# Two graph layers on one core: a deeper pipeline in the edge pass, another split of the last node update, and fewer waits of GpSimd on TensorE

## The reference

```python
# layer 0
msgs = z[dst] @ Wd + z[src] @ Ws + edge_weight[:, None] * ww + bm
agg = segment_max(msgs, dst)                       # 0 where a node has no edge
x = layernorm(x + (relu(z @ W1a + agg @ W1b + b1) @ W2 + b2))
# layer 1
h = x @ node_fc_W + node_fc_b
alpha = segment_softmax(sum(h[src] * h[dst], -1), dst)
beta = segment_softmax(sigmoid(relu(edge_mlp(edge_attr)) . W2 + b2), dst)     # three gates per edge
h_att = segment_sum(alpha * (h[src] @ node_att_W)) / 3
h_rel = segment_sum(sum_m beta_m * (h[src] @ rel_att_W_m)) / 3
h_out = where(deg > 0, relu(concat(h_att, h_rel) @ out_fc_W + out_fc_b), h)
x = layernorm(x + gate * h_out + (1 - gate) * x)   # gate = sigmoid(x @ gate_W + gate_b)
```

## Time and profile before

| what | value |
|---|---|
| median of 3 runs | 2750.39 us (2747.92 to 2776.14) |
| the profiled execution | 2757.0 us, of which the span 2755.3 us |
| mean granted clock of TensorE | 0.803 |
| busy shares | PE 67%, PEld 41%, DVE 49%, ACT 40%, POOL 60% |
| edge-run pass, gathers at line 209 | 40.35 to about 1203 us |
| edge pass, gathers at line 462 | 1342.83 to about 2613 us |

### The profile page before, as it was taken

How to read it: one execution, slowest core, us unless ns; L and a number is a source line. 1 busy time by engine, 2 the same in 40 slices (tenths; PEclk the granted TensorE clock), 3 DMA queues, 4 the chain that set the end, 5 groups by cost and what they waited for, 6 DMA issues and landing times. The chain is left out here.

```text
span 2755.3 us, 43228 instructions
## 1 busy us (share of the span) xinstructions
PE 1841.2 (67%) x9891; PEld 1141.9 (41%) x9891; DVE 1341.2 (49%) x5207; ACT 1113.2 (40%) x3305; POOL 1654.1 (60%) x1718
## 2 busy tenths in 40 slices
PE   4677777667677775656567776667766667766774
PEld 3222222222222221114356665656655556655674
DVE  4555555554344444324545454445444455444459
ACT  1233333333333333323444444444444444444455
POOL 3756666666677776636445655555555665555535
PEclk7789888988888898777777777777778877787777
DMA  8433333333333333323311212121112122122213
GB/s 232 171 102 124 105 120 107 122 105 124 100 122 103 109 120 108 122 63 93 111 41 51 50 51 52 48 51 52 48 51 52 51 52 52 48 53 51 51 43 99
DMA packets 115983, 235.04 MB, mean 85 GB/s; under 512 B 32909, under 2 KB 68230, under 8 KB 106422
## 3 DMA queue, kind: packets, MB, share of 16 engines
q0 software_dynamic: 52832, 109.39, 16.2%
q1 hardware_dynamic: 56522, 97.21, 9.6%
q10 hardware_dynamic: 6540, 27.42, 2.8%
HBM read 166.01 MB, written 67.89 MB: 85 GB/s over the span
## 5 line engine op out<-in xcount | busy, mean ns | idle before, releaser
L462 POOL DMA_INDIRECT d_region<-d_h,d_region x784 | 747.2, 953 | 552.0 <-issue 238.3
L209 POOL DMA_INDIRECT acc<-d_src_product,b_region x784 | 779.5, 994 | 383.8 <-issue 204.8
L642 PE MATMUL banks<-acc,b_region 64*128 64x512 f32 x1176 | 345.5, 695 | 296.6 <-ACT gate_col L747 159.6
L850 DVE SCALAR_TENSOR_TENSOR acc<-b_region,acc 128x128 f32<-128x128 f32 x784 | 270.4, 345 | 362.9 <-DMA acc<-d_src_product,b_region 333.1
L1570 DVE TENSOR_TENSOR acc<-acc,banks 128x160 f32 x784 | 252.2, 322 | 327.3 <-remote 133.0
L642 PEld LDWEIGHTS banks<-acc,b_region 64*128 64x128 f32 x1176 | 106.2, 204 | 493.2 <-ACT gate_col L747 186.0
L1369 PE MATMUL banks<-d_region 128*128 128x128 f32 x1568 | 303.2, 352 | 9.2 <-issue 9.2
L1372 PE MATMUL banks<-d_region,pick 128*128 128x128 f32 x1568 | 289.2, 344 | 4.7 <-issue 4.5
L1372 PEld LDWEIGHTS banks<-d_region,pick 128*128 128x128 f32 x1568 | 274.0, 260 | 6.6 <-issue 6.5
L1369 PEld LDWEIGHTS banks<-d_region 128*128 128x128 f32 x1568 | 266.3, 255 | 16.4 <-issue 11.0
L861 DVE SCALAR_TENSOR_TENSOR acc<-acc,b_region 128x128 f32<-128x128 f32 x784 | 269.2, 343 | 0.0
(11 more groups left out here) (262 smaller groups left out, 2471.5 us busy)
## 6 DMA issues: line engine op xcount, KB each, us to landing
d_runs<-acc SPq DMA_DIRECT2D x48, 1024.0 KB
acc<-ea ACTq DMA_DIRECT2D x25, 1024.0 KB
acc<-d_src_product,b_region POOLq DMA_INDIRECT x784
d_region<-d_h,d_region POOLq DMA_INDIRECT x784
d_region<-d_rel SPq DMA_DIRECT2D x49, 256.0 KB
hT<-xT SPq DMA_DIRECT2D x7, 448.0 KB, 6.9
d_src_product<-acc SPq DMA_DIRECT2D x7, 448.0 KB, 4.2
acc<-xrow SPq DMA_DIRECT2D x1, 3136.0 KB
```

Source lines behind the costliest of these rows:

```text
L209: pool.indirect_dma_start(self.rows[:, s, j, :], None, d["B"], bass.IndirectOffsetOnAxis(self.idx[:, k:k + 1], 0)).then_inc(self.gathered[ ...
L462: pool.indirect_dma_start(rows[:, s, :], None, table, bass.IndirectOffsetOnAxis(idx[:, s:s + 1], 0)).then_inc(gathered[q], 16)
L642: last = nc.tensor.matmul(bank[4 + n % 2 * 2 + h][:, :], wf[h * DE:(h + 1) * DE, m * P:(m + 1) * P], ea[h * DE:(h + 1) * DE, u % (2 * UC), ...
L850: nc.vector.scalar_tensor_tensor(rows[:, s, j, :], wwb, wgt[:, k:k + 1], rows[:, s, j, :], ALU.mult, ALU.add).then_inc(ch, 1)
```

## The change

It touches five places.

1. The edge pass: the sums of group q stand at the head of TensorE's round, and everything ahead of them works one group further ahead (rows of q+5, scores of q+4, spread of q+3, weights of q+2). ScalarE and VectorE follow, but ScalarE's rescale stays at q, and VectorE's gate weights stay at q+1 and its additions at q. The weights `wts` get four buffers where there were two, and to make room `rel` is held as bf16, which is converted in the tables phase.
2. The gathers of the edge pass: `LAG` is 4 where it was 3, and the wait on turned weights in the middle of a group is gone.
3. The gathers of the edge-run pass: the two looks are gone; `LEASH` is counted in groups and stands for the same wait.
4. The last node update: ScalarE scales one product, GpSimd adds only the bias, VectorE adds three products, and ScalarE does the norm with the mean and root that VectorE prepares.
5. The tables phase: one more copy on VectorE.

In the diff below the third and fourth hunks from the end are TensorE's and VectorE's rounds of the edge pass, the last two ScalarE's part of the last node update.

```diff
...
             pool.wait_ge(rows_turned, it * NG + (NG + q - LAG + 1 + NG))
             pool.wait_ge(idx_ready, it * NG + (NG + q + 1))
             pool.wait_ge(rows_used, it * NG + (NG + q + 1))
-            gathers(q, range(0, GJ // 2))
-            pool.wait_ge(weights_turned, it * NG + (NG + q - LAGW + 1 + NG))
-            gathers(q, range(GJ // 2, GJ))
+            gathers(q)
...
-LAG = 3
-LAGW = 6
+LAG = 4
-LEASH = 4
-LOOKS_FROM = 12
+LEASH = 8
...
-                u = g // 2
+                if g >= LEASH + 2:
+                    pool.wait_ge(dt, (g - LEASH) // 2)
                 for j in range(GJ):
-                    if u > LEASH and (g % 2, j) == (0, 0):
-                        pool.wait_ge(dt, u - LEASH)
-                    if u >= LOOKS_FROM and (g % 2, j) == (0, 3):
-                        pool.wait_ge(tm, M * u - 4)
-                    if u >= LOOKS_FROM and (g % 2, j) == (1, 2):
-                        pool.wait_ge(tm, M * u - 3)
                     runs.gather(pool, d, g, j)
...
+            c.add(nc.vector.tensor_copy(short_rel, rel))
...
-        wts = [ca(GJ * 4 * W).rearrange("p (j k w) -> p j k w", j=GJ, k=4) for _ in range(2)]
+        wts = [ca(GJ * 4 * W).rearrange("p (j k w) -> p j k w", j=GJ, k=4) for _ in range(4)]
...
-                if q + 4 < end:
-                    turn_rows(it, q + 4)
-                if 0 <= q + 3 < end:
-                    scores(it, q + 3)
-                if 0 <= q + 2 < end:
-                    spread(it, q + 2)
-                if 0 <= q + 1 < end:
-                    turn_weights(it, q + 1)
                 if q >= 0:
                     sums(it, q)
+                if q + 5 < end:
+                    turn_rows(it, q + 5)
+                if 0 <= q + 4 < end:
+                    scores(it, q + 4)
+                if 0 <= q + 3 < end:
+                    spread(it, q + 3)
+                if 0 <= q + 2 < end:
+                    turn_weights(it, q + 2)
...
-                if 0 <= q + 3 < end:
-                    lowest(it, q + 3)
-                    picks(it, q + 3)
+                if 0 <= q + 4 < end:
+                    lowest(it, q + 4)
+                    picks(it, q + 4)
                 if 0 <= q + 1 < end:
                     gate_weights(it, q + 1)
-                if 0 <= q + 2 < end:
-                    references(it, q + 2)
+                if 0 <= q + 3 < end:
+                    references(it, q + 3)
                 if q % half == 0 and 0 <= q < end - NG:
                     next_indices(it, q)
                 if q >= 0:
                     add_windows(it, q)
...
                 for b in range(z):
-                    for k, to in ((0, sA), (1, sB)):
-                        last = nc.scalar.activation(to[c % 2][:, b, :], bank_of(c, b, k), ACT.Copy,
-                                                    scale=rz[:, 4 * c + b, k:k + 1])
+                    last = nc.scalar.activation(sA[c % 2][:, b, :], bank_of(c, b, 0), ACT.Copy,
+                                                scale=rz[:, 4 * c + b, 0:1])
...
+            def norm(c):
+                z, n = widths(c)
+                act.wait_ge(sh, c + 1)
+                if c >= 2:
+                    act.wait_ge(ost[c % 2], 16 * (c // 2))
+                for k in range(z):
+                    last = nc.scalar.activation(y[c % 2][:, k, :], v[c % 2][:, k, :], ACT.Identity,
+                                                bias=nmean[c % 2][:, k:k + 1], scale=std[c % 2][:, k:k + 1])
+                last.then_inc(ln, 1)
```

More of the change, by code:

```diff
@@ L451, in iterations_but_one, with gather_rows, gathers @@
     return eng.value_load(t["nit"][0:1, 1:2], min_val=MINIT - 1, max_val=MAXIT - 1)
-def gather_rows(nc, pool, t, table, idx, rows, idx_ready, rows_used, rows_turned, weights_turned, gathered, after_first):
+def gather_rows(nc, pool, t, table, idx, rows, idx_ready, rows_used, rows_turned, gathered, after_first):
     rest = iterations_but_one(pool, t)
-    def gathers(q, part=range(GJ)):
+    def gathers(q):
         hold(pool)
-        for j in part:
+        for j in range(GJ):
             s = q * GJ + j
@@ L1618, in phase_nodes1 @@
         mv = [ca(4 * 2).rearrange("p (b s) -> p b s", b=4) for _ in range(2)]
-        std = [ca(4) for _ in range(2)]
+        std, nmean = ([ca(4) for _ in range(2)] for _ in range(2))
         bank = t["psum"]
@@ L1751, in _ @@
                     relu(n + 1)
+                if 0 <= n - 1 < NC4:
+                    norm(n - 1)
         @block.vector
@@ L1775, in join @@
                 dve.wait_ge(bi, c + 1)
[L1776 to L1785 removed]
+                for k in range(1, K):
+                    to, before = sA[c % 2], done if k > 1 else None
+                    done = []
+                    for b in range(z):
+                        if before:
+                            h_.wait(before[b])
+                        last = nc.vector.scalar_tensor_tensor(to[:, b, :], bank_of(c, b, k), rz[:, 4 * c + b, k:k + 1],
+                                                              to[:, b, :], ALU.mult, ALU.add)
+                        if k < K - 1:
+                            done.append(h_.add(last))
                 last.then_inc(pm, 1)
```

91 lines of the change are left out of this document (38 added, 53 removed).

## The result

The changed kernel takes 2932.9 us (median of 4 runs, 2932.1 to 2942.2) where the kernel before takes 2751.8 us beside it (2747.9 to 2776.1): a ratio of 1.0645, with a 95% interval of 1.0606 to 1.0685. It is 181 us slower; I had forecast 68. The forecast had the sign, and the measured time lies above its range.

A forecast was written before the change was run, and what follows sets the result against it. It took waits as the bound: others see finished TensorE work late while GpSimd gathers back to back. Edge pass +81, its end +5, edge-run pass -5, node update -14, tables +1: +68 on 2750 gives 2818 us, range 2695 to 2890.

The forecast's parts named there:

- The bound and the loop: Edge pass: waits bound it; the new order adds a loop of 4.4 us, 6.4 at the lower clock.
- Trains of four with 6.7 us a group: Edge pass: each delivery gives GpSimd credit for one group, so it issues four gathers in 6.7 us.
- the signs named for "right": Edge-pass profile: no middle stops, sums released by gate weights, additions without remote waits, index waits above 50 us.
- Mostly four: Edge-pass profile sign: GpSimd's gathers start in trains of mostly four, 6.7 to 6.9 us a group.
- The indices: Edge pass, every fourth group: VectorE writes indices some 3 us later; 0.2 us a group, bounds 0 and 0.75.
- Over the pass: Edge pass: 6.9 us a group against 6.46 over 184 groups, +81 us, bounds -48 to +173.
- The edge-run pass: First gather pass without looks: the remaining wait on dots makes the same stops; -5 us, bounds -20 to +20.
- After the last gather: Eight remaining edge-pass rounds, +5 us (0 to +17), then the last node update, -14 us.
- The node update: Last node update: VectorE loses 49 norms and gains 49 additions and small operations; -14 us, bounds -5 to -18.
- Longer trains: Edge pass: without a middle stop, trains of eight become the rule, 6.2 us a group; 2690 us, chance 0.20.
- no change: Edge pass: saved middle stops pay for later gate weights, 6.46 us a group stays; 2740 to 2755 us, chance 0.18.
- Much slower: Edge pass: every round needs separate deliveries for sums and scores, 7.6 us a group or more; about 2950 us, chance 0.12.

The follow-up runs named there:

- the windows with plain DMAs: Edge-pass gathers replaced by plain DMAs of the table's first 128 rows: kernel before 2197.4 us, changed 2423.1, changed with earlier indices and gate weights 2287.1.
- the slowest kernel: The changed kernel with VectorE making the gate weights a round earlier, indices left as in the changed kernel: 3047.5 us.

## Why the prediction was wrong

**The bound and the loop: right.** A wait bounds the edge pass, and the new order adds a loop from the scores over the lowest score and the gate weights to the sums. I forecast 4.4 us for it at full clock and 6.4 at the lower. Chips Q show it bare: 4.67 us in one stretch, 5.1 and 6.3 in another. Trains of four with 6.7 us a group were forecast; once the indices are out of the way, three of four groups have 6.6 us. Most of the signs named for "right" are there: no middle stops, sums released by gate weights (in part by the name of the copy that ends with them), waits for indices well above 50 us. "Mostly four" is half true: in the changed kernel every third train is of eight.

**The indices: the step that failed in the edge pass.** I wrote that they come some 3 us later, bounds 0 and 0.75 us a group, and took 0.2, "because the quiet saves the next stop of 1.7 us". Measured by moving them: 7.26 to 6.85 us, 0.41 a group, and the fourth group still loses 0.7 us against the others, another 0.2. That is 0.6 by the rates, across two chips; by the ratios of the times it is 107 / 184 = 0.58 and the 0.2, or 0.8. So the term lies near its upper bound. They wait for one delivery more than the sums do (GpSimd's stop before a fourth group is 4.4 to 7.0 us, the first of the pass left out, where the other stops are of 1.7 to 2.9 us), and the stop saved behind it does not pay for that. Over the pass: forecast +81, measured +151.6 us, within the bounds of -48 to +173. With 0.6 in place of 0.2 the indices alone make (0.6 - 0.2) x 184 = 74 us, as much as the 70 that are missing.

**The edge-run pass: the other step that failed.** Forecast -5 us (-20 to +20), measured +40 in the whole change, +29.5 alone, nothing on chips Q. The step was "the remaining wait on dots makes the same kind of stop, every second unit". It priced the pass by its stops alone, read from units up to about the 48th, and put a longer gather at nothing. Up to 700 us that holds: both kernels are equal (352 and 350 gathers). Later, where TensorE and VectorE do the nodes' work beside the units, the kernel without looks has few and long stops in place of many short ones, yet idles as long. What it loses there it loses in the gathers: over the pass they take 30.1 us more, the waits 4.6. I had named the late units, with bounds of -20 and +10 us. The 4 us more at the end (17.64 for 13.52) went the forecast's way, one more unit left over. That the looks keep the gathers short follows from the kernels with and without them; how they do it was not isolated.

**After the last gather: right.** Forecast +5 - 14 = -9, measured -15.9 us. Three rounds there take 2823.18 - 2806.48 = 16.7 us, 5.6 each against 4.3 in the earlier trace rows, between my 4.4 and 6.4:

```profile
2806.48 0.29 DVE L1507 CUSTOM_DVE_ANT_0 d_region<-d_region,banks 128x128 f32<-128x128 f32 x1 [1.96 <-PE banks L1349]
...
2823.18 0.29 DVE L1507 CUSTOM_DVE_ANT_0 d_region<-d_region,banks 128x128 f32<-128x128 f32 x1
```

The node update gave 16.6 us alone (forecast 14). The norms now stand on ScalarE, 49 of them at 0.49 us, and VectorE's products are 147 at 0.34 us. The small operation that I could only bound (0 to 0.34 us) takes 0.62 us, twelve times; the update could bear it.

```profile
L1784 DVE SCALAR_TENSOR_TENSOR g_region<-banks,g_region 128x128 f32<-128x128 f32 x147 | 39.0, 342 | 4.9 <-POOL g_region L1658 4.8
L1740 ACT ACTIVATE hT<-g_region 128x128 f32<-128x128 f32 x49 | 20.2, 487 | 1.1 <-DVE g_region L1810 0.9
...
L1810 DVE SCALAR_TENSOR_TENSOR g_region<-g_region 128x4 f32<-128x4 f32 x12 | 7.5, 625 | 0.4
```

**The books.** 70 us from the edge pass, 44 from what lies ahead of it, less 7 behind it: 107 us, and 7 from having added the sum to a median below the profiled time. That is the 115 us between 2818 and 2933.

**The rivals.** Longer trains and no change fell. "Much slower" had the number (2950), but not by its mechanism of a delivery for sums and another for scores in every round: the trains were of four and eight, and the second delivery was that of the indices, at every fourth group. "Waits without delays", which I gave 0.02, is what the kernel before does on chips Q: 5.07 us a group, 2294 us; but there, too, the new order was slower, since its loop at the lower clock is longer than the 5.0 us of gathers.

The range was too narrow for the sum of its own bounds: +173 in the edge pass and +20 in the edge-run pass, with the other terms, would have allowed 2750 + 173 + 20 + 5 - 14 + 1 = 2935. I cut it at 2890 by giving "much slower" 0.12.

## What to carry to other kernels

When one step of a round is moved, write down for each engine which operations now fall a round behind it, and look for those that feed a queue only now and then: a copy needed at every fourth group, moved from one delivery to the next, cost about half of this change. Taking one wait out of a round shows little where a second stands at the same distance (gate weights, then additions), and can be worse than nothing. Price a stop or a look in every stretch with other work beside it, not only where the pattern is cleanest. And when a pass grows, look at the length of its operations before its waits: GpSimd's stops in the edge-run pass changed their shape, and the time went into the gathers.

## What the hardware showed that I had not expected

The same kernel takes 17% less time in the sets on chips Q, and behaves otherwise in kind. On chips P (2752 to 2789 us, granted clock 0.80) TensorE's completions reach other engines late while GpSimd gathers back to back, 2.6 us in the row at 1574.20 above and 6.3 us in the earlier trace rows; on chips Q (2294 us, clock 0.87 to 0.88) ScalarE starts on the same rows 0.03 us after TensorE's end, with trains of 16 gathers in the changed kernel. There the edge-run pass takes 10.2 us a unit instead of 11.7, the looks at TensorE are worth nothing in the edge-run pass, and the edge pass runs at GpSimd's own 5.07 us a group. What makes a chip one or the other, or whether it is the chip at all, the runs don't show. The ratio of the change was nearly the same on both, 1.0645 and 1.0596, for different reasons: on chips P late indices and one group a delivery, on chips Q the loop over the gate weights.

The granted clock went with the idling of TensorE: 0.93 at 4.54 us a group, 0.88 at 5.11, 0.85 at 5.74 with the same work (the windows with plain DMAs), 0.71 in the slowest kernel. So where a loop made TensorE wait longer its granted clock was lower as well, and sums at the lower clock take 1.84 to 2.07 instead of 1.15 us.

A gather of GpSimd is not of one length. In the edge-run pass single ones take 1.5 to 5.2 us where most take 0.94, and there are more of them without looks: 28 instead of 16, 30 us over the pass.
